# A perceiver block in one kernel: the first heads' contexts rounded in two pieces, two low parts moved to VectorE, two means moved to other PSUM banks

## What is computed

```python
x = x + _L0_xattn_ref(_layernorm(x), ctx_2048, itok, W_kvc, W_dq, W_uq, W_qr, W_uk, W_kr, W_uv, W_o)   # a window of 9 context rows per token, 16 heads
x = x + _L0_attn_ref(_layernorm(x), Wq, Wk, Wv, Wo, lambda_init)                                       # differential attention, 16 heads
x = x + _L0_ffn_ref(_layernorm(x), w_gate_up, w_proj)                                                  # ternary weights
```

## Time and profile before

| | |
|---|---|
| median of 3 runs | 884.65 us (881.57 to 886.21) |
| the profiled execution | 886.28 us, of which the span from the first to the last instruction is 884.4 us |
| TensorE, VectorE, ScalarE, GpSimd busy | 804.7, 619.1, 489.7, 170.3 us |
| mean granted TensorE clock | 0.969 |
| chain that ended last | TensorE 79%, VectorE 13%, ScalarE 5% |

### The profile page before, as it was taken

How to read it: one execution, slowest core, us unless ns; L and a number is a source line. 1 busy time by engine, 2 the same in 40 slices (tenths; PEclk the granted TensorE clock), 3 DMA queues, 4 the chain that set the end, 5 groups by cost and what they waited for, 6 DMA issues and landing times.

```text
span 884.4 us, 13999 instructions
## 1 busy us (share of the span) xinstructions
PE 804.7 (91%) x5321; PEld 615.3 (70%) x5335; DVE 619.1 (70%) x1070; ACT 489.7 (55%) x818; POOL 170.3 (19%) x168
## 2 busy tenths in 40 slices
PE   3999999999799889999999998999977659999996
PEld 3897555677688668787878887534763537888885
DVE  6774876567866799999999987337798796333333
ACT  3565884223566687876787743445656635343431
POOL 3146540000155310000000000233122230211112
PEclk9999999999899889999999998999999978999999
DMA  8733566861123535434453005032024061212101
GB/s 310 259 109 123 187 216 215 290 235 55 60 90 125 170 123 167 145 97 127 134 165 97 27 25 162 32 118 96 25 79 164 28 223 64 72 49 72 47 1 47
DMA packets 49867, 106.80 MB, mean 121 GB/s; under 512 B 6714, under 2 KB 26098, under 8 KB 46220
## 3 DMA queue, kind: packets, MB, share of 16 engines
q1 hardware_dynamic: 48908, 95.33, 32.5%
q0 software_dynamic: 896, 10.62, 3.1%
HBM read 100.69 MB, written 5.25 MB: 120 GB/s over the span
## 4 chain that ended last, share of the span: by engine, by line
PE 79%; DVE 13%; ACT 5%; issue 2%; DMA 1%; SPq 0%; POOL 0%; ACTq 0%; DVEq 0%
PE banks L41 16%; PE banks L43 15%; PE banks L42 15%; PE banks L2277 6%; PE banks L412 3%; PE banks L1388 2%; PE banks L2307 2%; PE banks L1844 2%; PE banks L2308 2%; PE banks L1249 1%; PE banks L1418 1%; PE banks L2108 1%; PE banks L1391 1%; PE banks L2060 1%; PE banks L1269 1%
## 5 line engine op out<-in xcount | busy, mean ns | idle before, releaser
L157 POOL TENSOR_TENSOR w_low<-w_raw,w_high 128x256 fp32r<-128x256 f32 (+2 forms) x44 | 58.4, 1335 | 152.8 <-ACT w_high L153 151.0
L153 ACT CAST w_high<-w_raw 128x1024 fp32r<-128x1024 f32 (+2 forms) x74 | 56.8, 779 | 22.7 <-PE banks L43 22.5
L41 PE MATMUL banks<-da_xT_high,w_high 128*128 128x512 f32 (+1 forms) x136 | 53.0, 390 | 1.7 <-DVE da_xT_low L280 1.7
L41 PE MATMUL banks<-hf_xhh,w_high 128*128 128x512 f32 (+1 forms) x136 | 51.8, 381 | 0.6 <-DVE hf_xhl L3031 0.6
L43 PE MATMUL banks<-da_xT_high,w_low 128*128 128x512 f32 (+1 forms) x136 | 52.2, 384 | 0.0
L42 PE MATMUL banks<-da_xT_low,w_high 128*128 128x512 f32 (+1 forms) x136 | 52.0, 382 | 0.0
L43 PE MATMUL banks<-hf_xhh,w_low 128*128 128x512 f32 (+1 forms) x136 | 51.9, 381 | 0.0
L42 PE MATMUL banks<-hf_xhl,w_high 128*128 128x512 f32 (+1 forms) x136 | 51.7, 380 | 0.0
L2947 POOL TENSOR_TENSOR hf_hl<-hf_h,hf_hh 128x512 fp32r<-128x512 f32 x16 | 24.3, 1520 | 123.2 <-ACT hf_hh L3003 123.2
L3011 DVE TENSOR_TENSOR hf_downW_l<-dw_w,hf_downW_h 128x512 fp32r<-128x512 f32 x16 | 11.2, 699 | 50.7 <-ACT hf_downW_h L2963 50.7
L2277 PE MATMUL banks<-ff_xT_high,tw_guT 128*128 128x512 f16 x120 | 45.5, 380 | 0.0
(11 more groups left out here) (443 smaller groups left out, 2487.9 us busy)
## 6 DMA issues: line engine op xcount, KB each, us to landing
cs_rows<-in_ctx SPq DMA_DIRECT2D x24, 1024.0 KB, 5.1
tw_raw<-in_L_ffn_w_gate_up SPq DMA_DIRECT2D x16, 512.0 KB, 4.5
hf_raw<-in_L_ffn_W_up SPq DMA_DIRECT2D x16, 512.0 KB, 3.5
w_raw<-in_L_xattn_W_o SPq DMA_DIRECT2D x8, 512.0 KB
w_raw<-in_L_attn_Wq SPq DMA_DIRECT2D x8, 512.0 KB
w_raw<-in_L_attn_Wk SPq DMA_DIRECT2D x8, 512.0 KB
w_raw<-in_L_attn_Wv SPq DMA_DIRECT2D x8, 512.0 KB
w_raw<-in_L_attn_Wo SPq DMA_DIRECT2D x8, 512.0 KB
```

The source lines that it names most:

```text
L41: nc.tensor.matmul(out, a[0], b[0], start=start, stop=False)
L153: self.nc.scalar.copy(self.wh[k][:, 0:cols], self.raw[k][:, 0:cols]).then_inc(self.split_hi[k], 1)
L157: self.nc.gpsimd.tensor_tensor(self.wl[k][:, 0:cols], self.raw[k][:, 0:cols], self.wh[k][:, 0:cols].bitcast(F32), ALU.subtract).then_inc(s ...
```

## The change

There are three edits.

First, contexts in two pieces. In `r == 16` ScalarE casts, for heads 0 and 1, the tokens of the first 12 rounds (384 of 512); the cast of W_o's first piece moves to `r == 17`. VectorE makes the low parts of those 384 tokens at the end of its round 16. After the last round both engines do the other 128 tokens.

Second, low parts. GpSimd no longer makes those of slots 2 and 3 for iteration 0. VectorE makes slot 2's in iteration 0 ahead of slot 0's, and slot 3's at the end of iteration 0.

Third, means. In iteration 0 the means of steps 2 and 3 go to banks 4 to 7, back to back and without a wait for the copies of the values or for each other; step 4 keeps bank 0.

```diff
@@ class WindowAttention
+    EARLY_ROUNDS = 12
+    def early_tokens(self, t):
+        return t.rearrange("p (a n) -> p a n", a=2)[:, :, 0:16 * self.EARLY_ROUNDS]
+    def late_tokens(self, t):
+        return t.rearrange("p (a n) -> p a n", a=2)[:, :, 16 * self.EARLY_ROUNDS:]
@@ scalar
             if r == R:
+                act.wait_ge(self.o_out, self.EARLY_ROUNDS)
+                for h in range(2):
+                    nc.scalar.copy(self.early_tokens(self.on[0][0][h][:, :]), self.early_tokens(self.qa[:, :, h])).then_inc(self.oh_, 1)
+            if r == R + 1:
                 c.split_high(act, *self.slot_y(0, 0))
         act.wait_ge(self.o_out, R)
-        high_out(0, 0)
+        for h in range(2):
+            nc.scalar.copy(self.late_tokens(self.on[0][0][h][:, :]), self.late_tokens(self.qa[:, :, h])).then_inc(self.oh_, 1)
@@ vector
+        def low_part(part, n):
+            for h in range(2):
+                dve.wait_ge(self.oh_, n + h + 1)
+                v.tensor_tensor(part(self.on[0][1][h][:, :]), part(self.qa[:, :, h]), part(self.on[0][0][h][:, :].bitcast(F32)), ALU.subtract).then_inc(self.ol_, 1)
+            if r == R:
+                low_part(self.early_tokens, 0)
-        low(0, 0)
+        low_part(self.late_tokens, 2)
@@ DiffAttention, gpsimd
-    FIRST = (0, 2)
     def gpsimd_first(self, pool):
-        for k in self.FIRST:
-            self.c.split_low(pool, k, self.f[k] + 1)
+        self.c.split_low(pool, 0, self.f[0] + 1)
         pool.wait_ge(self.c.ln_xn, M * (self.ln.u + 1))
-        for k in (1, 3):
-            self.c.split_low(pool, k, self.f[k] + 1)
+        self.c.split_low(pool, 1, self.f[1] + 1)
@@ scalar
-            tw.scalar_wide(act, 3 * i + 2, 0)
+            tw.scalar_wide(act, 3 * i + 2, 0 if i else 4)
...
-                tw.scalar_wide(act, 3 * i + 3, 0)
+                tw.scalar_wide(act, 3 * i + 3, 0 if i else 6)
@@ vector
+            if i == 0:
+                low(2, self.f[2] + 1)
             if not last:
                 low(0, self.f[0] + 2 + i)
...
-            if i:
-                low(3, self.f[3] + 1 + i)
+            low(3, self.f[3] + 1 + i)
@@ tensor
-            pe.wait_ge(self.v_out, 4 * i + 4)
-            tw.tensor(pe, 3 * i + 2, 0)
-            if i:
+            if i == 0:
+                for s in (2, 3):
+                    tw.tensor(pe, s, 2 * s)
+            else:
+                pe.wait_ge(self.v_out, 4 * i + 4)
+                tw.tensor(pe, 3 * i + 2, 0)
                 project(i - 1)
-            if i < PAIRS - 1:
+            if 0 < i < PAIRS - 1:
                 pe.wait_ge(tw.wide_ok, 3 * i + 3)
                 tw.tensor(pe, 3 * i + 3, 0)
...
-            if i < PAIRS - 1:
+            if i == 0:
+                pe.wait_ge(self.v_out, M)
+                tw.tensor(pe, 4, 0)
+            elif i < PAIRS - 1:
```

More of the change, by code:

```diff
@@ L1190, in vector @@
                 v.tensor_tensor(s[:, :, :], s[:, :, :], mx[:, 2, :].unsqueeze(2).broadcast_to([P, 4, self.KEYS]), ALU.mult).then_inc(self.p_done, 1)
+            if r == R:
+                low_part(self.early_tokens, 0)
         def low(i, k):
             for h in range(2):
-                dve.wait_ge(self.oh_, 4 * i + 2 * k + h + 1)
+                dve.wait_ge(self.oh_, 2 + 4 * i + 2 * k + h + 1)
                 v.tensor_tensor(self.on[k][1][h][:, :], self.qa[:, :, i * 4 + k * 2 + h], self.on[k][0][h][:, :].bitcast(F32), ALU.subtract).then_inc(self.ol_, 1)
-        low(0, 0)
+        low_part(self.late_tokens, 2)
         def outputs(i, k, n):
@@ L1425, in values @@
             for h in range(2):
-                pe.wait_ge(self.ol_, 4 * i + 2 * k + h + 1)
+                pe.wait_ge(self.ol_, 2 + 4 * i + 2 * k + h + 1)
                 if n >= 2:
@@ L3238, in _ @@
                 window.gpsimd(pool, ch)
-                pool.wait_ge(window.ol_, 2 * PAIRS)
+                pool.wait_ge(window.ol_, 2 * PAIRS + 2)
                 ternary.gpsimd(pool)
```

## The result

The changed kernel takes 879.38 us (median of 8 runs, 877.57 to 881.41), the kernel before 884.73 on the same chip: ratio 0.9942, interval [0.9928, 0.9955], or 5.1 us less (4.0 to 6.4), where 3.8 were forecast. The profiled execution has a span of 877.2 instead of 884.4, 7.2 less. Of that 0.97 was there before any changed instruction ran: ScalarE's cast of W_o's piece starts at 231.50 before, the early casts in its place at 230.53 after, and round 16's L1179 at 232.84 before, its counterpart L1198 at 231.87 after.

What follows compares the result with a forecast made beforehand. TensorE bounds the kernel (79% of what ended last), so an edit pays only where TensorE waits. The terms 0.4 + 3.3 - 0.1 + 0.2 = 3.8 us take the median from 884.65 to 880.8, range 878.6 to 883.6.

Steps and rivals of the forecast that it cites:

- A gain of 0.4: First value product: VectorE's late low part ends 0.2 after GpSimd's, TensorE starts at 238.0; 0.4 us, range 0 to 1.2.
- The late low part behind GpSimd: Before the first value product: VectorE's late low part, held up by GpSimd's, ends near 237.8; leaves 0.4 us gain.
- the unhindered 1.2: First value product: if GpSimd does not hold up VectorE's late low part, TensorE starts at 237.2, 1.2 us gained.
- The forecast row: Sign before the first value product: late low parts end right behind GpSimd's L157 at about 237.7; product 0.4 us earlier.
- 3.3 less 0.1: Softmax of iteration 0 ends 3.3 us earlier without GpSimd's slot 2 low part; slot 3's on VectorE loses 0.1.
- the 0.8 that the prediction had for a clock that stays up: Iteration 0, softmax end to contexts: moving the means gains 0.8 us with clock up, 0 with it down; 0.2 taken.
- More comes out: Rival: VectorE's late low part precedes GpSimd's (0.8 us more), clock stays up at softmax's end (0.6 more): 879.4; chance 0.17.
- Its other half: The part of that rival at the end of iteration 0's softmax: the clock stays up, 0.6 us more.
- The second half gains nothing: Rival, normalisation's second half: L262's 2.73 is not GpSimd's doing, or VectorE stalls elsewhere as long: 884.1; chance 0.12.
- Part given back: Rival, after the second half's transposes: clock falls again, scores, values and exponentials late, 1.5 of 3.3 lost: 882.3; chance 0.18.
- The transfer queue: Rival, SyncE's queue: step 4's tile, behind slot 2's refill, lands at 320.3, everything 5.4 us late: 886.3; chance 0.06.
- Just enough, cost 0: Iteration 0: step 4's raw tile lands near 315, its cast would come at 314.9; no cost taken.

## Why the prediction was right, and where it was not

The mechanism held in both seams: in the two profiled executions the softmax of iteration 0 ends 4.3 and the contexts start 4.8 earlier (less the 0.97), where 3.7 and 3.9 were forecast. The sum was 1.3 us short: 5.1 measured, 3.8 forecast, the interval of the measured gain from 4.0 to 6.4. That it came so near is in part luck: edit 1 was put at 0.4 and measured 2.7 alone, edit 2 was put at 3.2 and measured 2.7, and the two errors pull in opposite directions. And the two profiled executions flatter the change: over all traces the first seam is 1.0 us shorter in the mean and the rest up to the contexts 2.3, which places 3.3 of the 5.1.

**Edit 1: the term that was mis-sized.** "A gain of 0.4" stood against 2.7 measured alone (one kernel, measured twice, intervals from 1.1 to 4.2 us) and 2.0 on top of edits 2 and 3. The instructions that it names are borne out. The late low part behind GpSimd, forecast at 0.4, gave 0.7 where the clock was up (the two traces with slot 3's cast in iteration 1); the unhindered 1.2 was 1.3 once GpSimd's low part came later. The forecast row, late low parts ending at 237.7, did not come in the changed kernel's trace, since there the clock fell as the last contexts began. By the rule of the Trainium skill (SBUF — State Buffer, "Who interferes with whom"), whoever issues first blocks the other; the traces agree: GpSimd was first at 235.56 and 235.31, and VectorE's low parts took 1.22 for two instead of 0.69, and 3.64 instead of 2.10. What the working left out is the clock. It counts at 2.4 GHz; in three of six traces without the split the clock had fallen by the last contexts and the seam was 0.4 to 0.9 longer, and in four of six with it the late low parts came free of GpSimd for the same reason. So the seam is 1.0 us shorter in the mean of the traces, not 0.4. The rest of the 2.7, about 1.7 us (0.1 to 3.2 by the intervals, with the 1.0 taken as it is), stays open: shown by the times, not by a trace. L262's 1.79 instead of 2.73 in the traces of edit 1 alone is not it, as far as is known, since it comes without edit 1 too, and the run that keeps the clearings away from it was 0.6 faster (between 0.5 slower and 1.9 faster). Nor does the part behind the contexts of iteration 0 depend on the edits: to the end it is 550.6 to 553.1 without edit 2 and 551.1 to 552.6 with it.

**Edit 2** was forecast at 3.3 less 0.1 and gave 2.7 (1.7 to 3.8) alone. L262 fell from 2.73 to 0.17 in the trace, the transposes took 1.06, their wait went, and the clock stayed up. In that execution the softmax ends 3.5 earlier than before, counted from the start of L262, where 3.3 were forecast. The forecast took the profiled execution's 2.73 for the rule; where L262 takes 1.79, 0.9 less is to be had, and the measured value lies below the forecast in that direction, as does the mean of the traces, 2.3. Slot 2's 1.23 is hidden on VectorE: L1706 at 310.05 still had 1.59 of waiting for ScalarE's cast in front of it. Slot 3's 1.23 in iteration 1 cost nothing that the times show.

**Edit 3**: 0.2 forecast, 0.35 measured, neither of which can be told from zero. In the changed kernel's trace the contexts start 1.32 behind the softmax's end instead of 1.82; but with edit 2 alone, without the means moved, it is 1.36, and with the means alone 1.82. The clock fell 0.6 us behind the softmax's end in the first, 1.3 behind it in the second, and with it in the third. So the 0.5 goes with the clock; that the means add to it isn't shown, and the 0.8 that the prediction had for a clock that stays up was not seen.

**The rivals.** "More comes out", 879.4, is where the median fell, but not by its mechanism: the late low part did get in freely in the profiled execution, but behind GpSimd and not before it, and only 0.5 came of it. Its other half, a clock still up at the end of the softmax (0.6 more), did come in that execution, with the 0.5 named above. "The second half gains nothing" is refuted by L262's 0.17. "Part given back" did not happen: ScalarE is busy 11.34 of 12.00 and the clock 1.00 in that window. The transfer queue was closer than its chance of 0.06: the cast of step 4's tile waited 0.51 in one trace with edit 2, 3.75 in another, and 1.5 to 2.1 as soon as ScalarE came a microsecond earlier. "Just enough, cost 0" was right for the changed kernel's trace, with no room behind it.

**The end.** The inner iterations did not grow. The offset between the traces moves again in and behind the last iteration, by 1.6 (from the last key copy to the feed-forward's normalised rows 27.07 instead of 28.69), and 0.8 of that returns until the end. Before, the clock fell at 539.6, during the last output product, for whose banks the additions wait; after, at 540.5, before the transposes behind them. The two traces of edit 1 alone have one of these lengths each (27.08 and 28.69), so this isn't the change's doing.

## What to carry to other kernels

A wait ahead of a stretch where TensorE is full is worth its length and, where it comes with a longer low clock, more: 1.23 us of new waiting went with 2.6 to 3.2 at the first seam in one trace, 1.01 with 1.4 in another. One trace of each kernel is a poor yardstick for half a microsecond: pool the traces of all variants that leave a seam alone, and compare those with the clock in the same state. Look for a small instruction with a long time in the rows, as L262 here, and ask what GpSimd does beside it; and look at it in more than one execution before its whole length is put into the sum. Moving a low part off GpSimd also moves the release of its buffer, and every load behind that one in the queue: check the margin of the first of them.

## What the runs showed of the hardware

A VectorE instruction of two values per partition (L262, one input) was held by GpSimd's low part, and in one execution by its clearings too, which read nothing: 0.17, 1.79 and 2.73 us. It is one of the shortest instructions in the seam, and in the trace of before it took longer than any other of VectorE's from the window attention's last addition to the second half's low parts (L280).

The clock's low stretch at the first seam did not have one length. Windows from 232 to 243, first of the changed kernel, then of edit 1 alone, then of the changed kernel with W_o's cast last:

```profile
232.00:243.00 11.00, 8.42 (x31) 6.47 (x30) 7.41 (x13) 8.02 (x13) 4.30 (x3) 0.69 0.20 61
```

```profile
232.00:243.00 11.00, 8.43 (x26) 6.70 (x25) 7.24 (x13) 8.03 (x12) 4.47 (x3) 0.53 0.22 61
```

```profile
232.00:243.00 11.00, 7.19 (x30) 5.26 (x30) 8.66 (x15) 8.53 (x14) 4.16 (x3) 0.67 0.10 28
```

By windows of one microsecond the clock was down from 233.3 to 240.1 in the first (6.8 us), from 232.3 to 242.5 in the second (10.2), with the same instructions there and the same waits but for 0.13. In the third it was 10.2 too, from 235.7 to 245.9, with 1.23 of waiting in it. At half clock two matmuls of 512 columns start 0.43 apart, at full clock 0.23, so 3.4 us more of it cost some 1.6. In the traces without new waits the stretch from the first value product to the first of the four additions is 50.95 with 3.2 us of low clock in it, 51.27 with 4.2, 51.59 with 4.9 and 52.08 with 6.0. Over a whole execution the clock is only a part of the scatter: in the three sets of runs of the kernel before (25, 26 and 35) a mean granted clock higher by 0.01 goes with a span 2.0 to 3.1 us shorter, with a correlation of only -0.53 to -0.67, and the two traces of edit 1 alone have mean clocks of 0.969 and 0.973 but spans of 881.0 and 881.2.
